# A graph layer's gathers on Trainium2: more hand-fetched rows on two queues, in larger number loads

## What is computed

```python
h   = relu(layernorm(x))                        # 12500 x 128
xp  = h @ lin1_w                                # 12500 x 128
C   = 0.5 * (cos(edge_weight * pi / 10) + 1)
W   = (ssp(edge_attr @ mlp_w1 + mlp_b1) @ mlp_w2 + mlp_b2) * C[:, None]   # 212500 x 128
msg = xp[src] * W                               # one gathered row of xp for each edge
agg = segment_sum(msg, dst, 12500)
out = x + (ssp(agg @ lin2_w + lin2_b) @ lin_w + lin_b)      # ssp(v) = softplus(v) - ln 2
```

## Time and profile before

| what | us |
|---|---|
| runs (three) | 2023.22, 2026.22, 2027.63; median 2026.22 |
| profiled execution, own time | 2022.45 |
| its span | 2020.7 |
| PE busy | 1341.8 (66%) |
| PE weight load busy | 1108.7 (55%) |
| DVE busy | 1048.1 (52%) |
| ACT busy | 792.7 (39%) |
| POOL busy | 1517.5 (75%) |
| 16 DMA engines | 202.33 MB at 100 GB/s |

### The profile page before, as it was taken

One profiled execution on the slowest core, in us unless ns is written; L12 is line 12 of the kernel. 1 busy time (PEld: TensorE's weight loads), 2 busy tenths in 40 slices (PEclk: granted clock), 3 DMA queues, 4 the chain that ended last, 5 costly groups with the idle time before them and its releaser, 6 DMA issues.

```text
span 2020.7 us, 48993 instructions
## 1 busy us (share of the span) xinstructions
PE 1341.8 (66%) x12880; PEld 1108.7 (55%) x12881; DVE 1048.1 (52%) x3153; ACT 792.7 (39%) x925; POOL 1517.5 (75%) x1611
## 2 busy tenths in 40 slices
PE   5577667776776777676666666666666666666666
PEld 5465556655555556555555555555555555555454
DVE  8664655555545555555544444444544444445454
ACT  5764333333434443433343333333333334333332
POOL 7777777777777777777777777777777777777775
PEclk9887888888888878888787888778877878887887
DMA  9633343333343344334333233333333333333322
GB/s 320 247 94 92 89 97 88 98 98 92 92 99 97 88 97 99 87 93 102 87 88 97 77 97 90 84 98 81 92 94 80 98 86 88 97 88 87 96 76 51
DMA packets 114579, 202.33 MB, mean 100 GB/s; under 512 B 36409, under 2 KB 69917, under 8 KB 114173
## 3 DMA queue, kind: packets, MB, share of 16 engines
q0 software_dynamic: 51392, 105.35, 21.6%
q1 hardware_dynamic: 55228, 91.86, 14.7%
q10 hardware_dynamic: 7680, 1.98, 0.7%
HBM read 186.25 MB, written 12.80 MB: 99 GB/s over the span
## 4 chain that ended last, share of the span: by engine, by line
POOL 38%; ACTq 19%; issue 18%; ACT 16%; PE 4%; DVE 3%; DMA 1%; DVEq 0%; SPq 0%; POOLq 0%
POOL XG L460 38%; ACTq L576 17%; ACT TB L593 5%; ACT TB L587 4%; ACT TB L590 4%; ACTq L565 1%; PE PW L878 1%; ACT XG L482 1%; DMA XG<-xp_scratch,IX 1%; PE PA L897 1%; DVE XG L776 1%; DVE TB L651 1%; DVE SCR L630 1%; PE PX L824 1%; PE PX L862 0%
## 5 line engine op out<-in xcount | busy, mean ns | idle before, releaser
L460 POOL DMA_INDIRECT XG<-xp_scratch,IX x1542 | 1455.6, 944 | 470.6 <-issue 463.0
L776 DVE SCALAR_TENSOR_TENSOR XG<-PW,CC,XG 128x128 f32<-128x128 f32 x1602 | 453.1, 344 | 435.3 <-DMA XG<-xp_scratch,IX 399.6
L587 ACT ACTIVATE TB<-PX 128x1024 f32<-128x1024 f32 x208 | 212.8, 1023 | 1039.8 <-PE PX L862 532.9
L875 PE MATMUL PW<-BPB,ones 128*128 128x512 bf16 x415 | 183.7, 443 | 563.3 <-DVE XG L776 558.8
L878 PEld LDWEIGHTS PW<-W,TB 128*128 128x128 f32 x3314 | 545.9, 234 | 20.0
L878 PE MATMUL PW<-W,TB 128*128 128x128 f32 x3314 | 548.9, 320 | 0.0
L731 DVE SCALAR_TENSOR_TENSOR TB<-PX,TB 128x1024 f32<-128x1024 f32 x208 | 254.2, 1222 | 347.1 <-ACT TB L593 336.5
L875 PEld LDWEIGHTS PW<-BPB,ones 128*128 128x128 bf16 x415 | 41.2, 99 | 674.2 <-issue 670.2
L897 PE MATMUL PA<-OH,XG 128*64 128x64 f32 x6408 | 296.1, 259 | 0.0
L897 PEld LDWEIGHTS PA<-OH,XG 128*64 128x64 f32 x6408 | 265.4, 171 | 31.3 <-issue 18.4
L862 PE MATMUL PX<-AT,W 51*128 51x256 f32 x1662 | 258.2, 432 | 2.6 <-ACT XG L482 2.6
(11 more groups left out here) (107 smaller groups left out, 538.1 us busy)
## 6 DMA issues: line engine op xcount, KB each, us to landing
HA<-xp_scratch ACTq DMA_DIRECT2D x3840, 0.5 KB
AT<-attr_b SPq DMA_DIRECT2D x104, 512.0 KB
HT<-xp_scratch SPq DMA_DIRECT2D x3092, 0.5 KB
XG<-xp_scratch,IX POOLq DMA_INDIRECT x1542, 2.7
AG<-zero SPq DMA_DIRECT2D x1, 6400.0 KB, 21.6
xp_scratch<-XG SPq DMA_DIRECT2D x24, 256.0 KB
XR<-x SPq DMA_DIRECT2D x24, 256.0 KB
out<-XR SPq DMA_DIRECT2D x24, 256.0 KB, 3.8
```

The source lines that it names most:

```text
L460: e.indirect_dma_start(XG[q % XG_N][0:p, k * D:(k + 1) * D], None, xp, bass.IndirectOffsetOnAxis(ap=IX[0:p, t0 + k:t0 + k + 1], axis=0)).t ...
L587: e.activation(T, PXP[pair % 2][:, :], ACT.Abs).then_inc(s_ab, 1)
L776: ins = e.scalar_tensor_tensor(out=G, in0=weights(q)[0:p, k * D:(k + 1) * D], scalar=CC[0:p, t0 + k:t0 + k + 1], in1=G, op0=ALU.mult, op1= ...
L875: e.matmul(P[0:p, 0:n * D], ones[:, 0:p], BP[0][:, 0:n * D], start=True, stop=False, skip_group_check=True)
```

## The change

Three things. SP's turn has 40 rows instead of 32, with their numbers in two loads of 20 instead of four of 8, and SI holds one row of numbers for each turn. ScalarE takes 24 and 20 rows by turns instead of 20 each time (PAIR_ROWS is the mean, 22), still with one load of numbers a pair; four instead of three rows go behind each of the first two passes, and the rest (16 or 12) behind the third. HQ and AQ follow from these numbers, and with them which tiles GpSimd leaves out. No arithmetic of the layer is touched.

```diff
-ROWS = 32
-NH = (NCH - 3 - 2) * ROWS // TILE
-HQ = {18 + (j + 1) * TILE * CHQ // ROWS: j for j in range(NH) if 18 + (j + 1) * TILE * CHQ // ROWS < NQ - 2}
+ROWS = 40
+TURNS = NCH - 3
+HQ = {18 + -(-(j + 1) * TILE // ROWS) * CHQ: j for j in range((TURNS - 2) * ROWS // TILE)}
+HQ = {q: j for q, j in HQ.items() if q < NQ - 2}
 HQ[NQ - 2] = len(HQ)
...
-PAIR_ROWS = 20
+PAIR_ROWS = 22
+ODD_ROWS = 20
...
-        SI = sb("SI", [NH, TILE], i32)
+        SI = sb("SI", [TURNS, ROWS], i32)
...
-            def fetch(a, b):
-                n = a
-                while n < b:
-                    j, p = n // TILE, n % TILE
-                    m = min(8 - n % 8, b - n)
-                    if p == 0 and j >= HT_N:
-                        e.wait_ge(s_sc, HAND[j - HT_N] + 1)
+            def fetch(turn):
+
+                for h in range(0, ROWS, ROWS // 2):
+                    n0 = turn * ROWS + h
+                    if n0 >= END:
+                        return
                     _, at = nc.values_load_multi_w_load_instructions(
-                        SI[j:j + 1, p:p + m], engines=[mybir.EngineType.SP], min_val=0, max_val=ROW * (NODES - 1),
+                        SI[turn:turn + 1, h:h + ROWS // 2], engines=[mybir.EngineType.SP], min_val=0, max_val=ROW * (NODES - 1),
                     skip_runtime_bounds_check_because="src holds node numbers, which are below NODES")
-                    for i, v in enumerate(at):
-                        e.dma_start(HT[j % HT_N][p + i:p + i + 1, :].bitcast(u8), row(v)).then_inc(s_r[j % HT_N], 16)
-                    n += m
+                    for n, v in zip(range(n0, END), at):
+                        j, p = n // TILE, n % TILE
+                        if p == 0 and j >= HT_N:
+                            e.wait_ge(s_sc, HAND[j - HT_N] + 1)
+                        e.dma_start(HT[j % HT_N][p:p + 1, :].bitcast(u8), row(v)).then_inc(s_r[j % HT_N], 16)
...
-                n0 = b * PAIR_ROWS
+                n0 = b // 2 * 2 * PAIR_ROWS + b % 2 * (2 * PAIR_ROWS - ODD_ROWS)
...
-                o = b % 2 * PAIR_ROWS
+                o, m = (2 * PAIR_ROWS - ODD_ROWS, ODD_ROWS) if b % 2 else (0, 2 * PAIR_ROWS - ODD_ROWS)
                 _, at = nc.values_load_multi_w_load_instructions(
-                    SA[b // 2:b // 2 + 1, o:o + PAIR_ROWS], engines=[mybir.EngineType.Activation], min_val=0,
+                    SA[b // 2:b // 2 + 1, o:o + m], engines=[mybir.EngineType.Activation], min_val=0,
...
                     e.activation(T, PXP[pair % 2][:, :], ACT.Abs).then_inc(s_ab, 1)
-                    fetch(3)
+                    fetch(4)
                     e.wait_ge(s_ab, pair + 1)
                     e.activation(T, T, ACT.Exp, scale=-1.0).then_inc(s_ex, 1)
-                    fetch(3)
+                    fetch(4)
...
                     numbers((i - FIRST) // 2)
-                    fetch(PAIR_ROWS - 6)
+                    fetch(len(held) - 8)
...
-        "src_h": _np.ascontiguousarray(tiles(g["src"]).T[[quad(q)[0] for q in HAND]]),
+        "src_h": turns(tiles(g["src"]).T[[quad(q)[0] for q in HAND]], TURNS, ROWS),
```

More of the change, by code:

```diff
@@ L423, in _ @@
                 load(k)
-                fetch(min(END, (k - AT_N) * ROWS), min(END, (k - AT_N + 1) * ROWS))
+                fetch(k - AT_N)
                 while c < NNC and (k - AT_N) * CHQ >= starts(c) + 6:
```

## The result

The changed kernel takes 2066.58 us (median of 4 runs), the kernel before 2024.72 us beside it: ratio 1.021, 95% interval 1.0187 to 1.0232. It is 42 us slower where 11 us less were forecast, and outside the range. The profiled execution took 2067.64 us, its span 2065.8 us.

A forecast was written before the change was run, and what follows sets the result against it. GpSimd's chain of gathers was taken to set the end; nine fewer gathers gave -11.2 us, with slots, SP and queue disturbance charged 0 and ScalarE's 9.0 us pair under its bound: 2026.2 to 2015.0 us, range 2010 to 2022.

The forecast's parts named there:

- 1533 gathers: GpSimd's chain: nine gathers fewer than 1542, at 1.249 us each, take 11.24 us off.
- one stop for a slot, at quad 27: GpSimd's gather for quad 27 needs quad 0's slot, free some 0.9 us early: charged 0, kept 0 to 3 us.
- SP's three row slots: SP's tile 3 may wait 1 to 3 us for its slot every fifth tile, hidden: charged 0, ends 0 to 2.
- The passes: A fourth row transfer beside ScalarE's first two passes adds 0.19 and 0.15 us, together 0.34 us a pair.
- The bound at which ScalarE sets the end: Until a ScalarE pair costs 9.22 us, nothing is lost and the gathers set the end; 9.0 us was forecast.
- Do the two queues disturb each other? I add nothing: ScalarE's rows issued beside SP's rows cost at most 0.008 us a row more, so nothing was added.
- The forecast's own sign of being wrong: Wrong if ScalarE's pairs pass 9.2 us, GpSimd gaps exceed 0.3 us after 140 us, or VectorE awaits hand tiles at the end.
- the number load: ScalarE's load of 24 numbers instead of 20 adds 0.22 us every second pair, 0.11 us a pair.
- Rival (1): ScalarE becomes the bound to the end and the kernel gets slower, 19 us per 0.1 us above 9.22; chance 0.11.
- Its mechanism: Each ScalarE row issued while SP is busy waits out one SP transfer, some 0.21 us: pair 9.37 us, end 2044.

The follow-up runs named there:

- SP's part: Kernel before with only SP's 40 rows a turn in two loads of 20, ScalarE as before: 2018.30 against 2025.62 us, ratio 0.9965.

## Why the prediction was wrong

**What held.** 1533 gathers at an unchanged 1.249 us. The last one starts 9.2 us earlier for 11.2: 0.3 us are a later start, 0.3 us one gather that took 1.24 us, and 1.5 us one stop for a slot, at quad 27, whose sums came 2 us later in this execution (pair 4 starts at 148.1 for 145.8). The stop was charged with 0 and given 0 to 3. SP's three row slots cost nothing in the end (0.8 us of waiting in all). The passes cost 0.18 + 0.19 us for the 0.34 that were forecast. The bound at which ScalarE sets the end, 9.22 us a pair, is confirmed from both sides: 9.13 and 9.15 leave the end alone, 9.27 moves it.

**The step that failed** is "Do the two queues disturb each other? I add nothing". It took 0.008 us a row from two groups of rows of before. That comparison was right for the rate of before, and it looked for the wrong thing: a dispute between two issues at the same moment. What acts is the sum of the rows of both queues over a turn, in front of one DMA engine. Before, 72 rows pass in 17.1 us, 4.2 a us, 5% under the ceiling of 4.4; the change asks for 84 in 18.0 us, 4.7 a us. At the 4.42 that SP's part shows they take 19.0 us, a pair of 9.50, which is what the first 92 pairs took. The forecast's own sign of being wrong, pairs over 9.2 us, is what came. Of the 0.5 us over the forecast (9.50 against 9.0 in the first 92 pairs) some 0.36 is this.

**A term that was too small** is the number load: 0.20 us a pair, not 0.11. The 24 numbers cost 0.32 more, not 0.22, and the 20 behind them 0.08 more than before, which I had at nothing. With the passes this brings ScalarE's own bill to 9.15, which alone would still have gained.

**The rivals.** Rival (1) happened in its effect, ScalarE as the bound to the end, at 0.11. Its price for a pair of 9.55 would be 2015 + 0.33 x 192 = 2078 us; measured 2067, since the last 11 pairs close faster than taken, (2045.0 - 1980.9) / 11 = 5.8 us and not 6.2, and 21 us follow the last first pass instead of 26. Its mechanism, each row waiting out one of SP's, was not what the trace shows: in the changed kernel the rows that ScalarE issues with none of SP's in the 0.34 us before take 253 ns on average between 300 and 900 us, no less than those issued beside one (247); before it is 233 and 228. The rule on the shared generator (Trainium skill, Perfetto Trace Analysis, "DMA Instruction — HWDGE (DVE, Sync)") speaks of a lock held during an issue. In this trace the issue takes 0.25 us, and the other 10.3 us until the row's end lie behind it, where that lock is not.

The Trainium skill, DMA: Bandwidth & Descriptors, "Why a DMA increments its semaphore by 16 and not by 1", says that a transfer whose slowest dimension allows no split runs on one engine, from these queues always the lowest-numbered. The trace agrees that it is one engine: each row has one data packet and one of 4 bytes, and the eight late packets of each block are one engine's share. The number of that engine it doesn't show.

Why 40 rows in loads of 8 wait only 6.9 us at 4.37 rows a us can be read from the waits. SP sets the pace there: it waits for TensorE 0.4 us between 300 and 900 us, and TensorE's first layer waits for a block of attributes, which in the changed kernel it never does. Its waits (who, for whom: total us, times, longest):

```profile
PE PX L865 <- DMA AT<-attr_b: 185.8, 51, 7.8
```

So SP itself holds the rate just under the ceiling.

## What to carry to other kernels

Two queues that each have room are not two resources if their transfers meet behind the issue: add up what both put in per microsecond and look how long a transfer takes from its issue to its end, while the issue itself still looks fast. Test the parts of a change alone and together; here -7, -3.5 and +42 us were all true. A limit worked out from the profile (9.22 us a pair) is worth as much as the term that is held against it, and the term that had no row at the new rate was the one to bound from above.

## What was not expected of the hardware

- Single-row transfers of 512 bytes from SP's and ScalarE's queues together did not go over 4.44 a us. Just under it the issue gets only 8 to 10% longer (230 to 248 or 252 ns on average), while the time from issue to end goes from 2.1 to between 10 and 12.5 us. A large transfer on the same queue waits with them: one sixteenth of each 512 KB block comes 9.5 us behind the rest.
- A load of numbers into registers takes 0.79 us for 8, 1.24 for 16, 1.46 for 20, 1.78 for 24, 2.13 for 32, but 4.68 us for 20 that start at word 22 of a row of 42, and 1.54 at word 24 of a row of 44.
